# Scatters tied one by one to TensorE's place, and a group count ahead of every second gather

## The reference

```
h = layernorm(x) * (1 + ca) + sa
x = x + ga * attention(h)          # 16 heads of 8, causal, rope
h = layernorm(x) * (1 + cb) + sb
x = x + gb * ffn(h)
# ffn: 160 experts, top 8 of sigmoid(h @ router.T + bias), weights normalised and times 2.5;
#      an expert is silu(h @ w_gate.T) @ w_down.T with 64 inner columns; plus one shared expert
```

## Time and profile before

| | |
|---|---|
| time, median of 3 runs | 2200.42 us (2197.68 to 2208.45) |
| profiled execution | 2189.18 us, span 2187.3 us |
| TensorE busy | 1379.2 us (63%) |
| VectorE busy | 1190.1 us (54%) |
| GpSimd busy | 1147.3 us (52%) |
| ScalarE busy | 757.6 us (35%) |
| mean granted TensorE clock | 0.746 |

### The profile page before, as it was taken

How to read it: one execution, slowest core, us unless ns; L and a number is a source line. 1 busy time by engine, 2 the same in 40 slices (tenths; PEclk the granted TensorE clock), 3 DMA queues, 4 the chain that set the end, 5 groups by cost and what they waited for, 6 DMA issues and landing times.

```text
span 2187.3 us, 33316 instructions
## 1 busy us (share of the span) xinstructions
PE 1379.2 (63%) x10342; PEld 692.4 (32%) x10342; DVE 1190.1 (54%) x4186; ACT 757.6 (35%) x1599; POOL 1147.3 (52%) x1190
## 2 busy tenths in 40 slices
PE   3568887877787787778778743877776777600000
PEld 1123333323332332333333311555454555400000
DVE  3657766677677676666767436433333333434333
ACT  0045444434444443344345411222544544400000
POOL 1101255555555554555465666001777777777776
PEclk9579778777877787777778856888878877755555
DMA  4594445454444445444444313999999999812211
GB/s 137 174 292 133 138 133 146 127 174 127 134 144 137 134 140 155 135 133 139 138 134 128 105 64 96 293 301 297 351 330 321 344 327 327 290 57 59 60 57 54
DMA packets 291644, 380.99 MB, mean 174 GB/s; under 512 B 46457, under 2 KB 175627, under 8 KB 291340
## 3 DMA queue, kind: packets, MB, share of 16 engines
q1 hardware_dynamic: 234508, 267.65, 40.7%
q0 software_dynamic: 32768, 67.17, 9.9%
q10 hardware_dynamic: 24192, 44.05, 5.4%
HBM read 218.52 MB, written 160.18 MB: 173 GB/s over the span
## 4 chain that ended last, share of the span: by engine, by line
PE 25%; POOL 21%; DVE 19%; DMA 12%; issue 10%; SPq 10%; ACT 2%; POOLq 0%; DVEq 0%; ACTq 0%
POOL vh L1392 17%; DVE masked L554 7%; SPq L1286 4%; PE bank L544 4%; DMA prob<-pages 4%; PE bank L693 4%; DMA km<-k_stacks 4%; SPq L479 3%; PE bank L424 3%; POOL pages L769 2%; DMA k_stacks<-k_part 2%; PE bank L630 2%; PE bank L868 2%; PE bank L490 1%; DMA pages<-h,pos_s 1%
## 5 line engine op out<-in xcount | busy, mean ns | idle before, releaser
L1392 POOL DMA_INDIRECT vh<-results,pos_all x512 | 506.1, 988 | 316.0 <-DMA results<-v_ext 161.3
L554 DVE CUSTOM_DVE_ANT_0 masked<-bank,cb_all 128x512 bf16<-128x512 f32 (+3 forms) x1024 | 444.6, 485 | 280.2 <-PE bank L544 277.9
L769 POOL DMA_INDIRECT pages<-h,pos_s x512 | 504.8, 986 | 165.0 <-issue 164.6
L657 ACT ACTIVATE prob<-bank 128x512 f32<-128x512 f32 x640 | 347.5, 597 | 410.7 <-PE bank L642 406.4
L544 PE MATMUL bank<-km,qm 64*128 64x512 bf16 (+3 forms) x1024 | 210.4, 361 | 171.3 <-DVE rmax L554 106.7
L1402 DVE TENSOR_TENSOR vh<-vh,wts_all 128x1024 f32<-128x1024 f32 x64 | 79.2, 1238 | 406.1 <-DMA vh<-results,pos_all 406.1
L693 PE MATMUL bank<-prob,v_ext 128*32 128x512 f32 (+3 forms) x2048 | 234.2, 539 | 2.0 <-ACT prob L657 2.0
L1310 PE MATMUL bank<-c_all,prob 128*128 128x128 f32 x672 | 135.1, 334 | 148.9 <-DMA prob<-pages 148.0
L630 PE MATMUL bank<-qe,ke 64*128 64x512 bf16 (+3 forms) x1024 | 161.1, 346 | 36.5 <-ACT prob L657 33.0
L544 PEld LDWEIGHTS bank<-km,qm 64*128 64x128 bf16 x1024 | 50.3, 99 | 333.3 <-DVE rmax L554 194.6
L1310 PEld LDWEIGHTS bank<-c_all,prob 128*128 128x128 f32 x672 | 86.7, 165 | 192.0 <-DMA prob<-pages 179.3
(11 more groups left out here) (187 smaller groups left out, 1850.8 us busy)
## 6 DMA issues: line engine op xcount, KB each, us to landing
prob<-wexp SPq DMA_DIRECT2D x672, 96.0 KB
pages<-free_rows SPq DMA_DIRECT2D x42, 1024.0 KB, 7.5
prob<-pages SPq DMA_DIRECT2D x168, 256.0 KB
results<-v_ext ACTq DMA_DIRECT2D x168, 256.0 KB
qm<-q_stacks SPq DMA_DIRECT2D x64, 256.0 KB, 3.4
km<-k_stacks SPq DMA_DIRECT2D x64, 256.0 KB, 4.7
qe<-q_stacks SPq DMA_DIRECT2D x64, 256.0 KB, 3.8
ke<-k_stacks SPq DMA_DIRECT2D x64, 256.0 KB, 4.5
```

Of the source, the lines that this page charges most:

```text
L554: last = e.tensor_tensor_reduce(out=masked[:, g % 2, c0:c0 + (i + 1) * P], in0=MX[g % 2][:, c0:c0 + (i + 1) * P], in1=mask_w[:, S - (i + 1 ...
L657: e.activation(prob[:, slot, :], ST[g % 3][:, :], ACT.Exp, scale=SCALE).then_inc(s_exa, 1)
L769: e.indirect_dma_start(out=pages, in_=h2[:, t, :], in_offset=None, out_offset=bass.IndirectOffsetOnAxis(ap=pos_s[:, t * TOPK + k:t * TOPK ...
L1392: e.indirect_dma_start(out=y8[:, i, k, :], out_offset=None, in_=results[0:ready * 4 * GRP * P, :], in_offset=bass.IndirectOffsetOnAxis(ap= ...
```

## The change

Two edits. The scatters of turns 2 to 15 go through a new helper `paced`, which puts a wait ahead of most of them: for a number of maximum or exponential units of the turn, read off the scatter's own place. The places of both groups move as well: the 14 from 0 to 0.44 to 0 to 0.4, the 18 from 0.54 to 0.99 to 0.52 to 0.98. In turn 16 the 14 stay as they were. In the gathers, every second one (k even) waits until `s_Y` shows a number of groups that rises by one every three gathers, from 40 up to 168; the waits that were there stay.

```diff
+        def paced(steps, i, start, end):
+
+            def step(e, f, at):
+                pairs, part = divmod(int(4 * UNITS * at) - 2, 2)
+                if pairs >= 0 and (part == 1 or i + 1 >= NB):
+                    wait(e, s_exp, 4 * UNITS * i - UNITS + 2 * (pairs + 1))
+                elif pairs >= 0:
+                    e.wait_ge(s_mxp, 4 * UNITS * (i + 1) + 2 * (pairs + 1))
+                f(e)
+            share = (end - start) / len(steps)
+            return [{"pool": lambda e, f=st["pool"], at=start + share * (k + 0.5): step(e, f, at)}
+                    for k, st in enumerate(steps)], start, end
...
-            if 3 <= i <= NB:
+            if 3 <= i < NB:
+                streams.append(paced(scatters(i - 3)[SHARE:], i, 0.0, 0.4))
+            if i == NB:
                 streams.append((scatters(i - 3)[SHARE:], 0.0, 0.44))
             if 2 <= i < NB:
-                streams.append((scatters(i - 2)[:SHARE], 0.54, 0.99))
+                streams.append(paced(scatters(i - 2)[:SHARE], i, 0.52, 0.98))
...
                 for k in range(TOPK):
+                    if k % 2 == 0:
+                        e.wait_ge(s_Y, min(NGRP, NE // GRP + (T * TOPK + k) // 3))
                     e.indirect_dma_start(
```

## The result

The changed kernel takes 2186.61 us (median; 2180.34 to 2193.51), the kernel before on the same chip 2200.42 (2188.59 to 2208.45). The ratio is 0.9942, with a 95% interval of 0.9923 to 0.9961: faster by 0.6%, which is 12.8 us by the ratio; the two medians lie 13.8 apart. The forecast was 2186 us.

The account below looks back on a forecast made before the run. The end was taken as the gathers' start plus 661 us plus some 8, the start hanging on shared waits in the turns. -17.6 + 2.3 + 1.0 = -14.3 us off the 2200.4 median gave 2186 us, range 2170 to 2207.

Parts of the forecast that it names:

- The mechanism: GpSimd's queue, turns 3 to 13: last of fourteen scatters goes ahead of `rest1` of q, so `pos_s` and h stop waiting.
- The removed wait: Turns 3 to 13, VectorE and ScalarE waiting for the last scatter: 1.6 us a turn saved, 17.6 us, bounds 0 and 2.3.
- The clock takes it back: Rival, TensorE in the turns: a lower granted clock cancels the freed wait; same, 2203.7 us, chance 0.29.
- All of it: Rival, turns 3 to 13: the full 2.3 us a turn is gained, with 5.5 us of transfers; 2171.9 us, chance 0.17.
- The turn's end: Store of k and next load of km amid scatters: at most 5.5 us to gain, taken as 0.
- Turn 15: Scatters there: `pos_s` 1.2 us late, one scatter fewer behind `rs`, one paced wait of 2.4; +2.3 us, between 0 and 4.
- The waits in the gathers: GpSimd, every second gather: 256 waits that never stand cost only handling, 0 to 2.6 us, taken as +1.0.
- The rival at 0.10 us a wait: Rival, GpSimd's gathers: 256 waits cost +25.6 us, making the kernel slower at 2210.7 us; chance 0.09.

Follow-up runs that it names:

- order alone: Kernel before with the fourteen scatters' places ending at 0.40 instead of 0.44 in turns 3 to 15, no waits added: 0.9923 (0.9994 on the 2597 us chip).
- gathers alone: Kernel before with only the 256 waits in the gathers added, scatters as before: 1.0001 (0.9781 on the 2597 us chip).
- many waits: Kernel before with four satisfied waits ahead of each of the 512 gathers, 2048 in all: 2194.73 us, 0.9988.
- waits at the old places: Changed kernel without the gathers' waits and with the scatters' old places, so only the scatters' paced waits are added: 1.0038 (0.9562 on the 2597 us chip).
- scatters alone: Changed kernel without the gathers' waits, so new places and paced waits of the scatters only: 0.9942 (0.9543 on the 2597 us chip).
- turn 15 free: Changed kernel without pacing in turn 15 and with the old end 0.44 for its fourteen scatters: 2181.38 us, 0.9919.
- Last two late: Kernel before with the fourteen's places ending at 0.48 in turns 3 to 15, so two scatters stand behind `rest1` of q: 2224.48 us, 1.0118.

## Why the prediction was right

**The mechanism held.** The last scatter behind `rest1` was the wait. It went by the order alone (0.9923), it did not go by pacing alone (1.0038), and it grew when a second scatter was put behind `rest1` (1.0118). The paced waits, the larger part of the diff, earned nothing on chips of this speed: the prediction priced them at nothing within the turns.

**The removed wait**, predicted at 1.6 us a turn or -17.6, bounds 0 and 2.3. One pair of profiles gives 1.05 a turn. Over the profiles on chips of this speed, turns 3 to 13 take 834.5, 838.0, 841.5 and 838.9 us where the wait is present (before, gathers alone, many waits, waits at the old places; mean 838.2), and 823.0, 822.8, 821.7, 825.6 and 825.6 where it is not (changed twice, order alone, scatters alone, turn 15 free; mean 823.7). That is -14.5 us, 1.3 a turn: nearer to VectorE's direct wait, 1.28, than to the 1.6 between VectorE's and ScalarE's. By these means the term was 3 us too large, though profiles with the wait lie up to 7.0 us apart and those without it up to 3.9, so 1.3 and 1.6 can't be told apart with certainty.

**The clock takes it back**: as a rival it was wrong in the whole; whether it was right in part is open. The mark at L811 did come 2.2 us sooner on average, as in turn 2, and 1.3 of it reached the end of the turn. The granted clock is 0.75 to 0.77 in the four profiles with the wait and 0.73 to 0.75 in the five without it; TensorE's busy time for the same 4677 matmuls has a mean of 654.9 us in the former and 667.7 in the latter. The Trainium skill (TensorE: Matmul & The Clock Gate, The HAM clock gate) has the monitor run free of the kernel, so that one kernel does not meet it alike each time. Like turns of one trace agree, at 0.79 and 0.76 in turns 7 and 10. It is tempting to say that a TensorE that waits less is granted less, but the tenth profile speaks against it. Last two late has the longest wait of all:
```profile
300.44:1167.04 866.60, 677.55 (x4676) 277.86 (x4677) 578.68 (x2552) 358.08 (x704) 439.70 (x462) 0.73 0.46 135
```
Its turns 3 to 13 have a clock as low as any, 0.73, and the busiest TensorE, 677.6 us. So what takes 0.9 of the 2.2 us back is not shown. "All of it" is excluded for the turns: of its 25.3 us at most 19.8 were freed, between the slowest profile with the wait and the fastest without it.

**The turn's end** at 0: the twelve loads of km ahead of turns 3 to 14 take 4.26 to 5.16 us in the changed kernel, mean 4.72, against 4.54 to 5.28, mean 4.87, before. That is 0.15 us a turn, already contained in the turns' 1.3; order alone, without the spacing, has 4.85.

**Turn 15** at +2.3, from its three pieces. Measured +2.0 (52.0 against 50.0); the wait of `pos_s` grew by 1.5 us instead of 1.2, and the gap of 2.55, less the 0.30 that stands between scatters anyway, is 2.25 instead of 2.4. `rs` (L832) came 11.3 us after `pos_s` in place of 11.85, so only 0.9 of the 1.5 us was passed on to it. The pieces then are 0.9 - 1.3 + 2.25 = 1.9. With turn 15 freed the interval does not tell the kernel from the changed one, but the trace does: 3.0 us less.

**The waits in the gathers** at +1.0, bounds 0 and 2.6. Measured 0: 1.0001 with 256, 0.9988 with 2048. The rival at 0.10 us a wait is excluded by far. The Trainium skill (Advanced Engine Details and Errata, Network/Comms) gives 50 to 100 ns for a sequencer's read of a semaphore; as a cost of these waits that is excluded too, for 2048 of them would be an estimated 102 to 205 us. As a time that a wait takes where nothing covers it, it is not contradicted: the one added wait of turn 15 goes with 0.06 us. The rival read its 0.10 from idle times behind instructions of different lengths, 0.47 behind 0.24 us of L1070 and 0.16 behind 1.15 us of L458, and that difference is not one of waits alone: behind a L1070 of 0.35 us the same scatter has 0.36. What failed in it is that a wait behind a running gather adds to the row at all.

**The sum by the measured terms** is -14.5 + 2.0 + 0 = -12.5 us. The forecast was -14.3, the measured ratio gives -12.8. The removed wait was taken 3.1 us too large, the two losses together 1.3 us; they partly cancel, and 2200.4 - 14.3 = 2186.1 against 2186.6 is closer than the terms are: that part is luck. The profiled execution of the kernel before also lay 11.2 us below its median, and the one of the changed kernel 1.6 below, so the sum rests on the means over profiles and not on the first pair.

## What to carry to other kernels

When a change moves instructions and adds waits, ask first where each one lands in its engine's queue: here one scatter ahead of, instead of behind, one 1.15 us vector operation was the whole gain, and it takes one number to get. Order alone (0.9923) and turn 15 free (0.9919) both have a lower ratio than the changed kernel (0.9942 and 0.995), though the intervals overlap. A satisfied wait behind a long instruction was free here, and one behind a short instruction went with 0.06 us. A wait that costs nothing and gains nothing on one chip may gain on another, so a part is judged on the chip it is meant for, beside the kernel before on the same one.

## What the runs showed of the hardware

- The kernel before takes 2195 to 2200 us in three of the four comparisons and 2597 in the other, on another chip, where the scatters' edits gain 4.6% and the gathers' 2.2%. With order alone there, the page's slices fall from 307 and 290 GB/s to between 165 and 182 in the six slices in which the gathers set in, where the changed kernel on its chip goes from 294 to 306 up to 321 to 342. ScalarE and VectorE stand for a releaser outside the core's engines and queues, up to 10.9 us at a time.
- Scatters of 128 rows in a row start 1.26 us apart, and the one behind `rest1` lets VectorE go 2.3 us after its start in ten of the eleven turns before and 3.0 in the other; with two behind `rest1` it is 2.3 in four turns and 3.3 to 4.3 in seven. Why is not known.
- A satisfied semaphore wait ahead of an indirect DMA on GpSimd, in a row of such DMAs of 0.94 us each, has no cost that 2048 of them would show. Behind a vector operation of 0.25 us, one wait more goes with 0.06 us from start to start (0.77 against 0.71).
- The same kernel's 512 gathers took 666.2 us from first to last start in one profile and 654.8 in another, with the same median of 0.94 to 0.95 us for one gather.
